# One scatter behind each causal mask and one per tile slot, in place of runs of four and pairs

## What is computed

```python
h = layernorm(x) * (1 + ca) + sa
x = x + ga * attn(h)                       # 16 heads of 8, causal softmax, layernorm, Wo
h = layernorm(x) * (1 + cb) + sb
bids = sigmoid(h @ conf_w.T + conf_b) * wealth
top_bids, experts = top_k(bids, 2); w = softmax(top_bids)
x = x + gb * sum_e w_e * (silu(h @ gate_e.T) * (h @ up_e.T)) @ down_e.T
```

## Time and profile before

| | |
|---|---|
| median of 3 runs | 680.74 us (672.39 to 682.2) |
| profiled execution | 685.81 us, span from first to last instruction 684.0 us |
| busy: TensorE / VectorE / ScalarE / GpSimd | 605.1 / 476.6 / 400.1 / 317.6 us |
| mean granted TensorE clock | 0.956 |
| attention steps | about 52 to 430 us |
| expert phase | about 430 to 660 us |

### The profile page before, as it was taken

The page is one execution under the profiler, slowest core; times in us unless marked ns, Lnnn a source line. Parts: engine busy times, 40 slices in busy tenths (PEclk is TensorE's granted clock), DMA queues, the critical chain, the costliest instruction groups (busy, mean ns, idle before and its releaser), DMA issues.

```text
span 684.0 us, 15710 instructions
## 1 busy us (share of the span) xinstructions
PE 605.1 (88%) x4889; PEld 411.6 (60%) x4890; DVE 476.6 (70%) x1592; ACT 400.1 (58%) x712; POOL 317.6 (46%) x447
## 2 busy tenths in 40 slices
PE   4789998999899899899899998799778999999940
PEld 1244544455445445455355453699778999999940
DVE  4797677678658658677687787477567666666636
ACT  1205677587666666766676667568434655665512
POOL 5103524254853753845645646535654333333325
PEclk9999999999989989999999999899989999999985
DMA  5723658535234234253333300111232111111128
GB/s 162 225 53 138 175 153 268 148 96 162 68 105 140 69 105 140 71 173 83 88 142 88 87 2 25 37 40 45 61 91 77 48 49 47 47 50 50 41 98 291
DMA packets 64899, 69.06 MB, mean 101 GB/s; under 512 B 8402, under 2 KB 55890, under 8 KB 64834
## 3 DMA queue, kind: packets, MB, share of 16 engines
q1 hardware_dynamic: 59938, 57.16, 28.7%
q0 software_dynamic: 4320, 8.99, 4.2%
q10 hardware_dynamic: 576, 2.10, 0.8%
HBM read 36.92 MB, written 31.03 MB: 99 GB/s over the span
## 4 chain that ended last, share of the span: by engine, by line
PE 76%; DVE 7%; DMA 5%; ACT 4%; issue 3%; POOL 2%; another core or an unknown queue 2%; SPq 1%; ACTq 0%; POOLq 0%; DVEq 0%
PE psN L739 17%; PE psO L522 11%; PE psN L491 11%; PE psT L505 10%; PE psO L750 9%; PE psN L493 4%; PE psM L530 2%; DMA kst_all<-k_parts_dram 2%; DVE negm L1101 2%; ACT probs L861 2%; PE psM L548 2%; PE psM L552 2%; DMA k_parts_dram<-kparts 1%; PE psM L570 1%
## 5 line engine op out<-in xcount | busy, mean ns | idle before, releaser
L1101 DVE TENSOR_REDUCE negm<-psN 128x1 f32<-128x512 f32 (+3 forms) x352 | 215.4, 637 | 85.4 <-PE psN L493 83.0
L861 ACT ACTIVATE probs<-psT 128x512 f32<-128x512 f32 x320 | 185.7, 598 | 84.5 <-PE psT L505 72.3
L491 PE MATMUL psN<-kst_all,qst_all 72*128 72x256 bf16 (+3 forms) x512 | 145.3, 321 | 10.1 <-DVE negm L1101 6.0
L739 PE MATMUL psN<-probs 128*128 128x128 f32 x1136 | 142.1, 279 | 4.8 <-ACT probs L978 2.3
L739 PEld LDWEIGHTS psN<-probs 128*128 128x128 f32 x1136 | 135.3, 195 | 5.3 <-issue 5.3
L505 PE MATMUL psT<-qst_all,kst_all 74*128 74x384 bf16 (+3 forms) x512 | 126.0, 308 | 9.0 <-ACT probs L861 7.9
L1593 POOL TENSOR_SCALAR_AFFINE_SELECT probs<-probs 128x512 f32<-128x512 f32 x128 | 79.6, 636 | 111.1 <-ACT probs L861 110.9
L1718 POOL DMA_INDIRECT expert_out<-kst_all,dest x71 | 69.2, 975 | 115.3 <-DVE kst_all L1496 112.7
L491 PEld LDWEIGHTS psN<-kst_all,qst_all 72*128 72x128 bf16 x512 | 52.3, 103 | 93.1 <-DVE negm L1101 44.8
L493 PE MATMUL psN<-maskts,identb 128*128 128x128 bf16 x512 | 105.3, 231 | 0.0
L522 PE MATMUL psO<-probs,vaug 128*32 128x512 f32 (+3 forms) x1024 | 99.9, 464 | 1.2 <-issue 1.0
(11 more groups left out here) (228 smaller groups left out, 716.6 us busy)
## 6 DMA issues: line engine op xcount, KB each, us to landing
q_parts_dram<-qparts SPq DMA_DIRECT2D x24, 384.0 KB, 3.4
k_parts_dram<-kparts SPq DMA_DIRECT2D x24, 384.0 KB, 3.2
qst_all<-q_parts_dram SPq DMA_DIRECT2D x32, 288.0 KB
kst_all<-k_parts_dram SPq DMA_DIRECT2D x32, 288.0 KB
kst_all<-dispatched SPq DMA_DIRECT2D x71, 66.0 KB
xall<-in_x SPq DMA_DIRECT2D x8, 256.0 KB, 4.1
gu_w<-in_gateT SPq DMA_DIRECT2D x4, 512.0 KB, 5.2
gu_w<-in_upT SPq DMA_DIRECT2D x4, 512.0 KB, 5.6
```

Source lines behind the costliest of these rows:

```text
L491: pe.matmul(psN[:, k % NBANKS, col:col + w], qst[g][0:KROWS, j, tb * P:(tb + 1) * P], kst[g][0:KROWS, j, 0:w], start=True, stop=False)
L739: mm = pe.matmul(bank[par][:, c * P:(c + 1) * P], ew[par][:, half, c * P:(c + 1) * P], xgT[par], start=True, stop=True)
L861: nc.scalar.activation(probs[:, g % 2, 512 * u:512 * (u + 1)], psT[:, u % TBANKS, :], ACT.Exp, scale=SOFTMAX_SCALE).then_inc(exp_done, 1)
L1101: nc.vector.tensor_reduce(dst, src, axis=AX.X, op=ALU.max, negate=True).then_inc(nat_done, 1)
```

## The change

`scatter(b, i)` now issues one indirect DMA, number i of the batch's eight (tile i // 2, expert i % 2). In step (b,2) one follows each of the four masks (i = 0 to 3), in step (b,3) likewise (i = 4 to 7). Before, four followed mask 0 of (b,2) and four came at that step's end, behind `add_attn`; of batch 5 these last four came behind all the steps. In the expert phase turns 10 to 17 have one scatter of batch 6 each and turns 18 to 25 one of batch 7, in place of two in each of turns 10 to 13 and 16 to 19. The number of scatters (64) and what they write is the same.

```diff
--- before.py
+++ after.py
@@ -1621,13 +1621,17 @@
                     hold("pool", pool, taken_chain, 5 * b + 2 + n)
                     gp.tensor_tensor(taken[:, n + 1], taken[:, n], both[:, n], ALU.add).then_inc(taken_chain, 1)
 
-            def scatter(b, tiles):
-
+            def scatter(b, i):
+
+                n, k = divmod(i, 2)
                 hold("pool", pool, r_chain, LINKS * (b + 1))
-                for n in tiles:
-                    for k in range(2):
-                        gp.indirect_dma_start(xd[:, :], bass.IndirectOffsetOnAxis(ap=slots_of(b)[:, k, n:n + 1], axis=0),
-                                              rows_of(b)[:, n, :], None).then_inc(dispatched, 16)
+                gp.indirect_dma_start(xd[:, :], bass.IndirectOffsetOnAxis(ap=slots_of(b)[:, k, n:n + 1], axis=0),
+                                      rows_of(b)[:, n, :], None).then_inc(dispatched, 16)
+
+            def scatter_step(b, g, c):
+
+                if g in (2, 3) and has_batch(b - 2):
+                    scatter(b - 2, TB * (g - 2) + c)
 
             def step(b, g):
                 if g == 0 and has_batch(b - 2):
@@ -1639,24 +1643,24 @@
                 mask(b, g, 0)
                 if g == 1 and has_batch(b - 1):
                     o_inv(b - 1)
-                if g == 2 and has_batch(b - 2):
-                    scatter(b - 2, (0, 1))
+                scatter_step(b, g, 0)
                 if g == 3 and has_batch(b - 1):
                     h_inv(b - 1)
                 mask(b, g, 1)
                 if g == 1 and has_batch(b - 2):
                     count(b - 2)
+                scatter_step(b, g, 1)
                 mask(b, g, 2)
+                scatter_step(b, g, 2)
                 if g == 0 and has_batch(b + 1):
                     low(b + 1, kres, kparts, k_mid, k_parts)
                 mask(b, g, 3)
+                scatter_step(b, g, 3)
                 if isinstance(b, int) and (b, g) == (0, 1):
                     x_inv(slice(2, B), 3)
                     x_shift(slice(2, B))
                 if g == 2 and has_batch(b - 1):
                     add_attn(b - 1)
-                if g == 2 and has_batch(b - 2) and not (isinstance(b, int) and b == B - 1):
-                    scatter(b - 2, (2, 3))
 
             x_inv(slice(0, 1), 1)
 
@@ -1686,7 +1690,6 @@
             low(1, qres, qparts, q_mid, q_parts)
             all_steps(step)
             L = B - 1
-            scatter(L - 2, (2, 3))
             h_scale(L - 1)
             o_inv(L)
             h_shift(L - 1)
@@ -1700,17 +1703,12 @@
                     h_shift(L)
                 if j == 8:
                     count(L - 1)
-                if j == 10:
-                    scatter(L - 1, (0,))
-                if j == 11:
-                    scatter(L - 1, (1,))
-                if j == 12:
-                    scatter(L - 1, (2,))
                 if j == 13:
                     count(L)
-                    scatter(L - 1, (3,))
-                if 16 <= j < 16 + TB:
-                    scatter(L, (j - 16,))
+                if 10 <= j < 10 + 2 * TB:
+                    scatter(L - 1, j - 10)
+                if 18 <= j < 18 + 2 * TB:
+                    scatter(L, j - 18)
 
             def send(i, u):
```

## The result

The kernel after took 659.47 us (median of 6 runs, 656.23 to 661.02), the kernel before 681.47 beside it on the same chip (672.39 to 687.46). The ratio is 0.973, 95% interval 0.966 to 0.980: faster. A ratio compares means, over the faster executions of a kernel and of the kernel before that ran with it, so it is not the quotient of the medians. The prediction was 660. The profiled execution took 658.68 us, its span 656.9.

A forecast was written before the change was run, and what follows sets the result against it. TensorE bounds the kernel and waits for signals that runs of indirect DMAs make late. The terms, 23.4 - 5 - 3.5 - 1 + 6.9 = 20.8 us, off the median of 680.7 gave 660 us; range 641 to 683.

The forecast's parts named there:

- Each scatter holds alone: Rival: each indirect DMA by itself delays signals, so spreading the scatters in attention makes it slower, 702 us; chance 0.07.
- Three still hold: Rival: groups of three at 1.91 us cost 16 us and dense expert-phase pairs 0.6 us per DMA, 683 us; chance 0.15.
- the turn of 4.38 us: Expert-phase turn by three indirect DMAs within 2.6 us, read as 1.6 us lost against 2.79 for an undisturbed turn.
- The scatters are innocent: Rival: attention steps are long for another reason, so only the costs in (c) and (d) remain, 685 us; chance 0.08.
- (a): Attention steps (2,2) to (6,3): the runs of four scatters cost 23.4 us that can go.
- (b): Attention: 10 groups of three scatters at 1.91 us still cost 0.5 us each, 5 us; bounds 0 and 16.
- (c): Steps (b,2): add_attn behind three more scatters delays VectorE about 0.7 us, 3.5 us lost over five batches; between 0 and 7.
- the pair at 1.79 us: Two sends in the expert phase, in a stretch of turns at 2.79 us each, read as costing 0.
- (d): Batch 7: eight scatters in its short steps make engines wait for GpSimd, 1 us lost; bounds 3 gained and 2 lost.
- (e): Expert phase: 14.6 us lost now, 7.7 after with scatter and send in pairs, 6.9 gained; bounds 14.6 better, 4.8 worse.

The follow-up runs named there:

- attn_only: Kernel after, but with the scatters of the expert phase in pairs as in the kernel before; 660.6 us against 684.13 for the kernel before, ratio 0.973.
- four_tiny: Kernel before with a GpSimd operation of 0.11 us between scatters of a run of four (pitch 1.26 to 1.59 us); 686.1 us against 684.13.
- four_spaced: Kernel before with a GpSimd operation of 0.73 us between scatters of a run of four (pitch 2.0 us); 701.28 us against 684.13.
- three_dense: Kernel after with one scatter behind mask 0 and three behind mask 3; 650.53 us against 653.91 for the kernel before, ratio 0.990.
- two_pairs: Kernel after with two scatters behind mask 0 and two behind mask 3; 654.67 us against 653.91 for the kernel before, ratio 1.000.

## Why the prediction was right, and where it was lucky

The **mechanism** held for the attention steps, on the chips on which the kernel before takes 680 us. Runs of indirect DMAs 1.27 us apart go with late signals to the other engines, and spreading them ends that. All work is kept in each of three kernels: in attn_only the whole loss of attention goes, in four_tiny it stays, and four_spaced shows for (b,2), and for it alone, that the pitch decides and not the order. The rivals fall there. *Each scatter holds alone* (702) asked for longer steps, all are at 10.59. *Three still hold* (683) asked for a loss behind the groups of three; at 1.82 us there is none. Its price had been misread: in the turn of 4.38 us ScalarE loads a table (493.63 to 494.91) and VectorE waits 2.58 us for its work behind that, and the same turn takes 3.65 us on chip 4, so at most 0.7 us of it is a hold. *The scatters are innocent* (685) falls with attn_only. By the rule of the Trainium skill behind that rival ("SBUF — State Buffer", "Who interferes with whom") nothing should have changed. The rule is about ports to SBUF. The trace of the kernel before on chip 4 agrees with it (10.59 us with four scatters over the step). On chips 1 and 2 engines do wait beside the same four (12 to 17 us a step); whether at a port or elsewhere no run shows. What differs between the chips no run shows.

Term by term:
- (a), what the runs of four cost: 23.4 us. The kernel before took 274.38 us from (2,0) to (7,3) on chip 1 and 250.53 on chip 4 (146.04 to 396.57), so 23.9. Right. The difference between the kernel before and the kernel after on chip 1 is the same 23.9.
- (b), 5 us for groups of three, and (c), 3.5 us for the late add_attn: both 0. The steps are 10.59 us, and from (2,0) to (7,3) the kernel after takes 250.51 us on chip 1 and 250.77 on chip 4. In (b) I took a value between two bounds; the nearer row, the pair at 1.79 us, had said 0, and the farther one, the turn of 4.38 us, shows 0.7 us of hold at most. In (c) the wait came (0.3 us in place of 0.7), but TensorE had slack for it. Together 8.5 us too much.
- (d), 1 us in batch 7: 1.2. Right in size and in mechanism: 3.2 lost to GpSimd's queue, 2.0 given back by the hold.
- (e), 6.9 us gained in the expert phase: 3.9, and by the comparison with chip 4 through another mechanism. The term was all hold: 14.6 us lost before, 7.7 after. Set against chip 4, the runs show 8.1 and 8.6. The 14.6 was too high twice. It allowed 0.75 us for rank and count_all; the turns of the kernel after without a hold take 53.10 us, 18 x 2.79 = 50.2, so that work takes 2.9. And it held 4.3 us that the same turns lose on chip 4 to GpSimd's late count, without any hold. The pairs, which were to let go before the next pair, closed up into fours, so the holds stayed. What was gained there is the wait for count, which the prediction does not name.

The sum of the terms was 20.8 us, the measured ones make 26.6, with the 0.3 us ahead of step (2,0) 26.9. Counted from the profiled execution (685.8) the forecast was 665.0, and 658.7 came: 6.3 too little off. It hit the median because I took the 20.8 from the median of the runs shown, 5.1 lower. That step hid the error. The profiled execution of before was likely long because it had dear holds, and the change takes those of attention away, so what was over the median went with them. No second trace of before on chip 1 can show that; what shows is that the kernel after ran within 656 to 661 us in its six runs on chip 1.

What was wrong in kind is the reach of the claim. I read the hold as a trait of the program; it is one of the program and of something that differed between the groups, most simply the chip. On chip 4, where the kernel before takes 654 us, the same change is worth 0.2% (-0.3 to +0.6).

Open: whether it is the chip or the time of the run that brings the hold; whether three scatters at 1.27 us hold on a chip like 1 or 2, and what an extra run costs there, since these kernels met chips without a hold; and where the signals are held. Every run here was recorded, so whether the hold is there without a recording is open too.

## What to carry to other kernels

When two engines that wait for different things start together, at a fixed distance behind the last of several indirect DMAs, spread the DMAs until they start about 1.8 us apart (the least pitch that was seen here to cost nothing), on an engine that has room for it; put them behind work that is there anyway, not behind a filler, or the masks of somebody else come late. Look afterwards whether the queue closed up again, and what stands behind a long row of DMAs on that queue: here TensorE waited for `count` even where nothing was held. And before a gain of this kind is believed or a theory thrown away, run the unchanged kernel beside it on every chip: here 27 us hung on the chip (or on the time of the run), more than on the change.

## What the runs showed of the hardware

- One program, 681 to 684 us on chips 1 and 2 and 654 on two others. Between the two traces of the kernel before (spans 684.0 and 651.5) 23.9 us lie in steps (2,0) to (7,2), 2.0 in batch 7's end and 8.1 in turns 12 to 30, all stretches with runs of indirect DMAs; the rest differs by 1.4 us the other way.
- On the chips with the hold, records of landed DMAs are missing. Counted in the trace, the semaphore of the 64 scatters should be raised 1024 times. Recorded are 405 (before) and 776 (after) on chip 1 and 412 to 691 on chip 2, but 997 to 1024 in the eight traces of chips 3 and 4. Signals and records get lost or late at the same places, which points to one crowded path, but is no proof. The page's list of DMA issues has a quicker sign: the line of the sends, first of the kernel before on chip 1, then on chip 4 (the last number is the median time to landing):

```profile
expert_out<-kst_all,dest POOLq DMA_INDIRECT x71
```
```profile
expert_out<-kst_all,dest POOLq DMA_INDIRECT x71, 2.3
```

  The time is missing in all six traces of chips 1 and 2 and there in all eight of chips 3 and 4. On other lines of the list it can be missing without a hold: that of the tile loads in three_dense, that of the scatters on chip 4.
- A send (64 KB) lands 2.3 us after its issue on chips 3 and 4, a scatter 2.5 us after it in two_pairs, the one trace that has the number; both are somewhat over the 2.0 us at which the waits ended. The Trainium skill ("DMA: Bandwidth & Descriptors", "Anatomy of one DMA — SWDGE (gpsimd) path") gives 2.0 us plus the bytes at 436 GB/s: 2.15 for 64 KB (an estimate), so the trace is near it.
- VectorE's small tensor_tensor at 176.07 in four_spaced took 2.50 us in place of 0.17, beside three masks and add_attn of GpSimd (175.49 to 178.54), and ended 0.03 us after the last of them. It took 2.36 in the other four steps (b,3) of that run, and 1.59 in (2,3) of two_pairs, where it ended with add_attn. By the Trainium skill ("SBUF — State Buffer", "Who interferes with whom") a VectorE instruction with two SBUF inputs contends with a GpSimd instruction that reads SBUF; this row agrees.
